# The last product before a graph layer's second half, by column parts

## The reference

```python
def gat_layer(x, W, a_s, a_d, b, edge_index, concat):
    h = (x @ W).reshape(n, H, C)
    alpha_s = jnp.einsum('nhc,hc->nh', h, a_s)
    alpha_d = jnp.einsum('nhc,hc->nh', h, a_d)
    e = jax.nn.leaky_relu(alpha_s[src] + alpha_d[dst], NEG_SLOPE)
    m = jax.ops.segment_max(e, dst, num_segments=n)
    e = jnp.exp(e - m[dst])
    denom = jax.ops.segment_sum(e, dst, num_segments=n)
    alpha = e / (denom[dst] + EPS)
    out = jax.ops.segment_sum(h[src] * alpha[:, :, None], dst, num_segments=n)

x = x + gat_layer(elu(gat_layer(norm(x), W1, ...)), W2, ...)   # relu in layer 1
```

## Time and profile before

| | us |
|---|---|
| three runs, median | 1182.47 |
| the profiled execution | 1183.24 |
| its span | 1181.4 |
| TensorE busy in the span | 1129.0 (96%) |
| VectorE busy | 581.0 (49%) |
| ScalarE busy | 455.9 (39%) |
| mean granted clock of TensorE | 0.991 |

### The profile page before, as it was taken

The page is one execution under the profiler, slowest core; times in us unless marked ns, Lnnn a source line. Parts: engine busy times, 40 slices in busy tenths (PEclk is TensorE's granted clock), DMA queues, the critical chain, the costliest instruction groups (busy, mean ns, idle before and its releaser), DMA issues.

```text
span 1181.4 us, 15711 instructions
## 1 busy us (share of the span) xinstructions
PE 1129.0 (96%) x6363; PEld 722.7 (61%) x6363; DVE 581.0 (49%) x890; ACT 455.9 (39%) x521; POOL 22.3 (2%) x48
## 2 busy tenths in 40 slices
PE   8899999899999999999999999999999999989998
PEld 6677785776755455536777686555665555445543
DVE  7977744746644334303565774454544543232310
ACT  4765514533533233202353564343434432222210
POOL 2000010000000000000000000000000000000000
PEclk9999999999999999999999999999999999999999
DMA  9998565948999999999685598999999999999996
GB/s 384 423 421 350 211 249 221 388 186 357 402 419 430 427 427 428 427 421 424 260 333 205 221 399 328 428 429 427 427 429 428 427 427 427 428 427 428 427 426 285
DMA packets 45399, 443.34 MB, mean 375 GB/s; under 512 B 5088, under 2 KB 5248, under 8 KB 11920
## 3 DMA queue, kind: packets, MB, share of 16 engines
q1 hardware_dynamic: 42336, 427.05, 87.0%
q0 software_dynamic: 2992, 15.29, 3.3%
HBM read 441.93 MB, written 0.39 MB: 374 GB/s over the span
## 4 chain that ended last, share of the span: by engine, by line
PE 75%; DMA 12%; DVE 5%; ACT 4%; SPq 2%; issue 1%; POOL 0%; DVEq 0%; ACTq 0%
PE PJ L2087 15%; PE PJ L2056 11%; DMA ring<-in_weights 8%; PE AC L2124 8%; PE TP L2146 8%; PE PJ L2065 6%; DMA extra<-in_weights 3%; PE AC L1847 2%; SPq L663 2%; PE MS L1659 2%; PE AC L1860 2%; PE PJ L2047 2%; PE TP L2097 2%; DMA scratch<-in_weights 1%; PE TP L2015 1%
## 5 line engine op out<-in xcount | busy, mean ns | idle before, releaser
L2087 PE MATMUL PJ<-ring,picked 128*64 128x512 f32 (+1 forms) x588 | 149.7, 594 | 0.0
L942 ACT ACTIVATE low<-PJ 128x512 f32<-128x512 f32 x51 | 30.2, 592 | 251.1 <-PE PJ L2087 179.9
L1416 DVE SCALAR_TENSOR_TENSOR act<-low,CB,PJ 128x512 f32<-128x512 f32 x51 | 38.0, 746 | 159.3 <-PE PJ L2056 83.7
L2087 PE MATMUL PJ<-scratch,picked 128*32 128x512 f32 (+1 forms) x360 | 106.9, 594 | 1.8 <-DMA extra<-in_weights 1.8
L2146 PE MATMUL TP<-ring,extra 128*64 128x512 f32 (+3 forms) x384 | 102.1, 488 | 1.0 <-issue 0.5
L1434 DVE TENSOR_TENSOR ring_lo<-ring,w_lo_u 128x1536 fp32r<-128x1536 f32 x40 | 69.2, 1756 | 49.8 <-ACT w_lo_u L959 49.8
L2146 PE MATMUL TP<-scratch,extra 128*64 128x512 f32 (+3 forms) x320 | 86.0, 488 | 0.0
L959 ACT ACTIVATE w_lo_u<-ring 128x1536 fp32r<-128x1536 f32 x40 | 58.1, 1484 | 63.2 <-PE AC L2124 29.3
L2087 PEld LDWEIGHTS PJ<-ring,picked 128*64 128x64 f32 (+1 forms) x588 | 42.7, 124 | 55.6 <-issue 54.9
L1434 DVE TENSOR_TENSOR ring_lo<-ring,w_hi_u 128x1536 fp32r<-128x1536 f32 x34 | 58.9, 1755 | 25.2 <-ACT w_hi_u L959 24.8
L2065 PE MATMUL PJ<-ring_lo,XTh 128*128 128x512 f32 x168 | 66.5, 396 | 0.0
(11 more groups left out here) (471 smaller groups left out, 2245.3 us busy)
## 6 DMA issues: line engine op xcount, KB each, us to landing
ring<-in_weights SPq DMA_DIRECT2D x147, 1536.0 KB, 17.0
scratch<-in_weights SPq DMA_DIRECT2D x73, 1536.0 KB, 19.0
extra<-in_weights SPq DMA_DIRECT2D x39, 1536.0 KB, 20.5
extra<-in_attn POOLq DMA_DIRECT2D x11, 768.0 KB, 10.5
ring<-in_weights SPq DMA_DIRECT2D x8, 768.0 KB, 28.5
extra<-in_attn POOLq DMA_DIRECT2D x6, 512.0 KB, 10.4
extra<-in_weights SPq DMA_DIRECT2D x4, 768.0 KB, 24.5
ring<-in_weights SPq DMA_DIRECT2D x8, 384.0 KB, 16.4
```

What stands on the lines that cost most here:

```text
L942: A(silu, PJ[:, 0:SEG], ACT.Silu).then_inc(S("silu_ready"), 1)
L1416: v.scalar_tensor_tensor(hexp, silu, weight, PJ[:, SEG:2 * SEG], ALU.mult, ALU.mult) \
L2087: ins = mm(dst[c], x[:, t, c], slab_at(LOAD[q, kind, side])[:, t * SEG:(t + 1) * SEG], start=(t == 0), stop=(t == KT - 1))
```

## The change

At the last segment of the three first attention layers (c = 0, 2 and 5), `product2` runs all its matmuls for columns 0 to 511 first and then those for columns 512 to 767; for c = 2 this holds for tiles 2 and 3 only. Between the parts it raises a new semaphore, `first_part`. VectorE forms both sums over the first 512 columns after that, into the new tile `part`, raises `first_terms`, and after the whole product forms them over the last 256 columns with `part` as the starting value. ScalarE copies 512 columns after `first_terms` and 256 after `vectors_used`. `keep_warm` and all that follows on TensorE are as before.

```diff
+SECONDS = (1, 3, 6)
...
             def second(c):
+                act.wait_ge(S("first_terms"), SECONDS.index(c) + 1)
+                A(hs2[:, 0:SEG], AC[:, 0:SEG], ACT.Copy)
                 act.wait_ge(S("vectors_used"), GAT[c]["unit"] + 1)
-                copy_h2()
+                A(hs2[:, SEG:D], AC[:, SEG:D], ACT.Copy).then_inc(S("h2_copied"), 1)
                 exps(c, 0)
                 turned(c, 0)
...
             def second(c):
+                u = GAT[c]["unit"]
+                dve.wait_ge(S(f"vectors_loaded_{u % 2}"), 16 * (u // 2 + 1))
+                dve.wait_ge(S("first_part"), SECONDS.index(c) + 1)
+                for side in range(2):
+                    ins = v.tensor_tensor_reduce(out=junk[:, 0:SEG], in0=AC[:, 0:SEG],
+                                                 in1=AB[:, u % 2, side * D:side * D + SEG], scale=1.0, scalar=0.0,
+                                                 op0=ALU.mult, op1=ALU.add, accum_out=part[:, side:side + 1])
+                    if side == 0:
+                        then(ins)
+                ins.then_inc(S("first_terms"), 1)
+                dve.wait_ge(S("first_terms"), SECONDS.index(c) + 1)
                 name, value = multiplied(c - 1, FIRST[c - 1]["segs"] - 1)
                 dve.wait_ge(S(name), value)
-                terms(GAT[c]["unit"], [0], D, AC)
+                for side in range(2):
+                    ins = v.tensor_tensor_reduce(out=junk[:, SEG:D], in0=AC[:, SEG:D],
+                                                 in1=AB[:, u % 2, side * D + SEG:side * D + D], scale=1.0,
+                                                 scalar=part[:, side:side + 1], op0=ALU.mult, op1=ALU.add,
+                                                 accum_out=al[:, side, 0:1])
+                    if side == 0:
+                        then(ins)
+                ins.then_inc(S("vectors_used"), 1)
+                dve.wait_ge(S("vectors_used"), u + 1)
...
                 if c == 5 and graph_split(j):
                     s = graph_number(False, j)
+                    if j == last:
+                        for part, (a, b) in enumerate(halves()):
+                            for t in range(4):
+                                hi = graph_hi(s, t // 2)[:, t % 2 * D:(t % 2 + 1) * D]
+                                lo = slab_lo(n)[:, t * D:(t + 1) * D]
+                                if part == 0 and t % 2 == 0:
+                                    pe.wait_ge(S("graph_lo"), 2 * (NARROW_SLABS + s) + t // 2 + 1)
+                                for x, w in ((xl, hi), (xh, lo), (xh, hi)):
+                                    ins = mm(AC[:, a:b], x[:, t * P:(t + 1) * P], w[:, a:b], start=False,
+                                             stop=(t == 3 and x is xh and w is hi), skip_group_check=True)
+                                if part and t % 2:
+                                    ins.then_inc(S("graph_used"), 1)
+                            if part == 0:
+                                ins.then_inc(S("first_part"), 1)
+                        return
...
+                    if j == last:
+                        early, late = halves()
+                        steps(2, (0, 1, 2), (early,))
+                        steps(3, (0, 1, 2), (early,)).then_inc(S("first_part"), 1)
+                        steps(2, (0, 1, 2), (late,))
+                        steps(3, (0, 1, 2), (late,)).then_inc(S("graph_used"), 1)
+                        return
```

More of the change, by code:

```diff
@@ L370, in gnn_ffn_kernel @@
         mv = sb("mv", [P, 2])
+        part = sb("part", [P, 2])
         veps = sb("veps", [P, 2])
@@ L1810, in product2 @@
                                 ins = mm(AC[:, a:b], x[:, t * P:(t + 1) * P], w[:, a:b], start=False,
-                                         stop=(j == last and t == 3 and x is xh and w is hi), skip_group_check=True)
+                                         stop=False, skip_group_check=True)
                         if t % 2:
@@ L1816, in product2, with steps @@
                 if c == 2:
-                    def steps(t, of):
+                    def steps(t, of, parts=halves()):
                         w = slice(t * D, (t + 1) * D)
@@ L1822, in steps @@
                             x, wt = ((xh, lo), (xh, hi), (xl, hi))[step]
-                            for a, b in halves():
+                            for a, b in parts:
                                 ins = mm(AC[:, a:b], x[:, t * P:(t + 1) * P], wt[:, a:b],
@@ L1851, in product2 @@
                     ins.then_inc(S("plain_used"), 1)
+                    return
+                if j == last:
+                    for part, (a, b) in enumerate(halves()):
+                        for t in range(4):
+                            k = 2 * split_number(n) + t // 2
+                            hi, lo = half_split(k)
+                            if part == 0 and t % 2 == 0:
+                                pe.wait_ge(S("split_lo"), k + 1)
+                            for x, w in ((xl, hi), (xh, lo), (xh, hi)):
+                                ins = mm(AC[:, a:b], x[:, t * P:(t + 1) * P], w[:, t % 2 * D + a:t % 2 * D + b],
+                                         start=False, stop=(t == 3 and x is xh and w is hi), skip_group_check=True)
+                            if part and t % 2:
+                                ins.then_inc(S("split_used"), 1)
+                        if part == 0:
+                            ins.then_inc(S("first_part"), 1)
                     return
```

## The result

| | runs | median, us | range, us |
|---|---|---|---|
| before | 20 | 1181.07 | 1177.79 to 1184.19 |
| changed | 20 | 1185.16 | 1181.61 to 1188.18 |

The ratio is 1.0035, with a 95% interval of 1.0026 to 1.0044. The changed kernel is slower by some 4 us; 1180.8 was forecast, and the time lies outside the range (1178.0 to 1183.9). The profiled execution took 1186.39 us.

A forecast was written before the change was run, and what follows sets the result against it. The prediction took TensorE to bound the kernel, with three quarters of the chain. Gains of 0.62 + 0.39 + 0.62 = 1.63 us turn the profiled 1183.24 into 1181.6, less 0.77 to the median: 1180.8 us, range 1178.0 to 1183.9.

The forecast's parts named there:

- VectorE's start and sums: At the hand-overs, sums start before the product ends; 0.69 us per 512-column part, 0.42 per 256-column part.
- E: Start of the first warming matmul behind the last product matmul, layers 0, 1, 3 (first to third place): 151.35, 245.93, 641.13 us.
- the other end: Second sums' starting value read from a column: priced 0, with 0.1 us for each of two as upper bound.
- 256s by themselves: Last product's 256-column matmuls back to back: 0.12 us each, 12 at first and third place, 6 at second.
- the rival of slow ones: Back-to-back 256-column matmuls in the product take 0.22 us each: net +1.1 us, 1183.6; chance 0.07.
- The term rows: TensorE's term rows after the warming matmuls: start E+1.79 at first and third place, E+1.91 at second.
- the cover: 16 warming matmuls ahead of the term rows, 1.79 us, hide VectorE's later finish at the first and third place.
- The three gains: Hand-overs in layers 0, 1 and 3 shorten by 0.62, 0.39 and 0.62 us, sum 1.63.
- No instruction is slower, no bytes are added: After the third place, the transfers' long busy stretch starts earlier by the same amount, so the gain reaches the end.
- places that are 0.6 shorter and a span that isn't: Sign of a wrong forecast: hand-overs 0.6 us shorter, but the whole span not shorter.
- the end is set by transfers: Weight stream leads between the places, gains become waits: 0 to 0.6 us left, 1182.2; chance 0.10.
- The clock: TensorE's low-clock stretches, up to 1.7 us each, may move: 1177.5 with two gone, 1182.5 with one more; chance 0.15.

The follow-up runs named there:

- the five pairs: Kernels with the change against kernels without it, weight buffers at the same places: ratio to before differs by -0.0013 in the mean, 1.5 us.
- pad_only: Kernel before plus the unused 8-byte tile `part` where the change allocates it, moving `scratch` on by 32 bytes: ratio 1.0042 to before.
- weights_moved: Kernel before plus an unused 8-byte tile just ahead of `scratch`, moving it by 32 bytes while the small tiles stay: ratio 1.0051 to before.
- all_moved: Kernel before plus an unused 8-byte tile ahead of `ring`, moving all 15 weight buffers and small tiles by 32 bytes: ratio 1.0027 to before.

## Why the prediction was wrong

- **VectorE's start and sums.** Right in kind. The first sum started at E-1.12 and E-0.39 (E-1.24 and E-0.52 were forecast), and a first part takes 0.69 as said. A second part takes 0.48, not 0.42: of the 0.1 given as the other end for a starting value read from a column, 0.06 is there. Ready at E+1.37 and E+2.09 (read-outs done), instead of E+1.13 and E+1.85.
- **256s by themselves.** 12 of them stand between 149.92 and E at 151.35, 0.12 each, as taken; the rival of slow ones is out. (At the second place the last 512 lets VectorE start 0.72 earlier than before by the forecast's own numbers, half of the first place's 1.44; the forecast calls it two thirds. Its sum doesn't use that figure.)
- **The term rows.** E+1.78 at the first place (E+1.79 forecast): the cover was there. E+2.15 at the second, not E+1.91, because VectorE was later by 0.24: 0.13 at its start and 0.06 in each of two sums.
- **The three gains.** 0.68 + 0.20 + 0.68 = 1.56 against 0.62 + 0.39 + 0.62 = 1.63, and 1.5 us in the whole time by the five pairs. So the mechanism of the hand-over was right.
- **The failed step** is the sentence "No instruction is slower, no bytes are added", and with it that the long busy stretch "starts earlier by the same amount" and so ends earlier. It starts earlier, and then lasts longer. The forecast priced the tile `part` at nothing without asking where it lies and what lies behind it. Its real price is that of pad_only: 0.42%, 4.5 us at medians of 1184.81 and 1180.36 (in the pair of traces of before and changed the packets give 2.8 + 1.5 = 4.3). The forecast's last sign of being wrong, "places that are 0.6 shorter and a span that isn't", is what came, but not for the reason that it was written for: no gain turned into a wait.
- **The rival "the end is set by transfers"** was weighed by the chain's 12%. That was the wrong row. The chain puts the time on TensorE as long as a matmul is running; whether a stretch is paced by transfers is told by the DMA share and rate of that stretch. Before, it was:

```profile
300.00:540.00 240.00, 237.29 (x1436) 127.10 (x1436) 83.53 (x63) 72.70 (x73) 1.11 (x2) 1.00 1.01 422
900.00:1050.00 150.00, 146.14 (x966) 82.06 (x964) 59.67 (x44) 48.30 (x45) 0.00 (x0) 1.00 1.01 428
```

  A mean share of 1.01 over 150 us and more means that the 16 DMA engines are full all the time, and then a packet that is 0.5% slower should make the stretch 0.5% longer (428 GB/s became 425 in pad_only), though TensorE is busy for 146 of 150 us too. With this row read, transfers still wouldn't have taken the hand-over's gain (the restart moves with it, and in five pairs it arrives), but anything that touches the buffers would have had to be priced.
- **The clock.** Its low stretches moved, but ahead of the restart there are three in either execution. The third stands at 579 us in the one of before, where it cost the 1.69 us shown above, and at 657 in the one of after, where it cost nothing: from the third statistic to the restart it is 13.86 us in both.

```profile
579.30:582.70 3.40, 3.40 (x7) 1.81 (x6) 3.16 (x9) 3.38 (x3) 0.00 (x0) 0.50 0.00 0
```

```profile
657.10:660.50 3.40, 3.40 (x5) 1.34 (x5) 2.96 (x16) 3.38 (x3) 0.00 (x0) 0.50 0.00 0
```

  So the clock made the first trace pair look better ahead of the restart than it was. It is not the cause of the loss: pad_only has that over 12 runs against 24, at a mean granted clock of 0.9947 against 0.9942.

## What to carry to other kernels

Where a stretch shows a DMA share of 1.0, the transfers pace it whatever the chain says, and the start addresses of the buffers they fill are part of the design: keep each at a multiple of 256 bytes in the partition (measured here for one kernel and for packets of 12,288 bytes). A new tile, however small, is an edit to the address of all that is allocated behind it; put it last, or compare the addresses of before and after. When a time moves and no instruction does, compare the rate and the packets, and try the added allocation by itself, unused. And where two traces differ by a microsecond or two at some point, compare the stretches of low clock ahead of it before calling that a gain or a loss.

## What the runs showed of the hardware

**The start of the buffers moves their packets' time.** With all 15 buffers at multiples of 256, 0.976 of the 12,288-byte packets took 460 ns or less; 32, 64 and 128 bytes past it are about alike (fast share 0.34, 0.31, 0.35 with `scratch` off). The Trainium skill, "DMA: Bandwidth & Descriptors", section "How a descriptor splits into AXI transactions", says that a transaction must start at a 256-byte boundary and that a descriptor that starts elsewhere fetches from the boundary below. It says this of what a transaction reads; here the buffers are what the transfers write. The runs agree on the step of 256 bytes. They do not agree on a price that grows with the distance: by the page's counts, estimated, 32 bytes past would cost 1 beat of 384 and 128 bytes 4, and here they cost 2.4 and 2.1 ns in the mean (461.05 to 463.43 and 463.17, packets under 475 ns).

**It spreads.** Only 6 of 15 buffers were moved in weights_moved, but the fast share fell from 0.765 to 0.344, by more than these buffers' part, since `scratch` takes 73 of the 259 transfers. The landing time rose for `ring` and `extra` as well (17.0 to 17.5, 20.5 to 20.9 us, in the changed kernel), which waiting behind slower packets could also do. And with all of them off by 32 more (all_moved) the mean is no worse than with `scratch` off alone. How packets to different buffers slow each other was not taken apart, and stays open.

**A sum with its starting value in a column took 0.06 us more than expected.** Over 256 columns it takes 0.48 us, where the sums with a constant (0.96 for 768 columns, 0.69 for 512) give 0.42 along a line. No run has a 256-column sum with a constant, so that the column is the reason is an inference.
